# Selecting source rows with wide one-hot streams and a transpose, for fifteen groups of edges

## Time and profile before

| | |
|---|---|
| Time, median of 3 runs | 1214.72 us (1213.41 to 1215.13) |
| Span of the profiled execution, first to last instruction | 968.1 us |
| The profiled execution's own time | not given apart; the median stands for it, which leaves 246.6 us around the span |
| TensorE (PE) busy | 920.9 us, 8724 matmul passes |
| VectorE (DVE) busy | 504.3 us |
| ScalarE (ACT) busy | 247.8 us |
| GpSimd (POOL) busy | 375.2 us |
| Mean granted TensorE clock | 0.978 of 2.4 GHz |

### The profile page before, as it was taken

One profiled execution on the slowest core, in us unless ns is written; L12 is line 12 of the kernel. 1 busy time (PEld: TensorE's weight loads), 2 busy tenths in 40 slices (PEclk: granted clock), 3 DMA queues, 4 the chain that ended last, 5 costly groups with the idle time before them and its releaser, 6 DMA issues.

```text
span 968.1 us, 22399 instructions
## 1 busy us (share of the span) xinstructions
PE 920.9 (95%) x8724; PEld 699.7 (72%) x8724; DVE 504.3 (52%) x1959; ACT 247.8 (26%) x434; POOL 375.2 (39%) x398
## 2 busy tenths in 40 slices
PE   4888999999899999999889999999999999999995
PEld 2644555555454465555589999999998998999994
DVE  8699999993211111121267554554654553644541
ACT  3667677772010111001101111111111111110211
POOL 1000000000000000111277777777777777777771
PEclk9979999999999999999989999999999999999997
DMA  4300100102000000000084444444443443533430
GB/s 129 73 2 12 14 2 13 13 13 65 1 1 1 1 1 7 15 11 12 21 188 141 129 118 119 129 119 115 131 123 104 128 130 107 150 108 107 127 99 30
DMA packets 47481, 67.99 MB, mean 70 GB/s; under 512 B 15793, under 2 KB 26252, under 8 KB 47244
## 3 DMA queue, kind: packets, MB, share of 16 engines
q1 hardware_dynamic: 35852, 42.90, 16.0%
q0 software_dynamic: 11520, 23.62, 9.4%
HBM read 63.18 MB, written 3.30 MB: 69 GB/s over the span
## 4 chain that ended last, share of the span: by engine, by line
PE 84%; DVE 11%; ACT 1%; issue 1%; DMA 1%; SPq 0%; ACTq 0%; DVEq 0%
PE f_ps L1185 26%; PE f_ps L1236 25%; PE f_ps L1290 12%; PE f_ps L1221 10%; DVE f_region L611 2%; DVE f_region L609 2%; PE f_ps L1070 2%; PE f_ps L1063 2%; PE f_ps L1160 2%; DVE f_region L615 2%; DVE f_region L613 2%; PE f_ps L1122 1%; PE f_ps L1081 1%; PE f_ps L1258 1%; PE f_ps L1262 1%
## 5 line engine op out<-in xcount | busy, mean ns | idle before, releaser
L559 POOL DMA_INDIRECT f_adj<-table,f_table_idx x360 | 353.7, 982 | 110.0 <-issue 108.5
L1185 PE MATMUL f_ps<-f_adj,f_parts 125*128 125x500 fp8e4 (+1 forms) x1575 | 333.3, 353 | 0.1
L1236 PE MATMUL f_ps<-f_parts 125*128 125x128 bf16 x4200 | 250.7, 220 | 4.0 <-DVE f_parts L801 4.0
L1236 PEld LDWEIGHTS f_ps<-f_parts 125*128 125x128 bf16 x4200 | 244.0, 98 | 11.1 <-issue 8.7
L1185 PEld LDWEIGHTS f_ps<-f_adj,f_parts 125*128 125x128 bf16 x1575 | 144.0, 97 | 131.0 <-issue 13.0
L544 POOL TENSOR_TENSOR f_rest<-f_region,f_parts 125x512 f32<-125x512 f32 (+1 forms) x7 | 7.3, 1049 | 462.2 <-ACT f_parts L1028 462.2
L940 ACT CAST f_adj<-f_ps 128x500 f32 x213 | 125.9, 591 | 55.5 <-PE f_ps L1070 39.6
L1290 PE MATMUL f_ps<-f_adj 128*128 128x94 f32 (+20 forms) x984 | 128.0, 275 | 3.5 <-ACT f_adj L1050 3.5
L1290 PEld LDWEIGHTS f_ps<-f_adj 128*128 128x128 f32 x984 | 118.3, 192 | 6.0 <-issue 5.8
L781 DVE TENSOR_SCALAR f_adj<-f_iota,f_dst_abs 128x94 f32<-128x94 f16 (+4 forms) x416 | 87.7, 284 | 65.0 <-PE f_ps L1290 65.0
L1221 PE MATMUL f_ps<-f_We,f_region 128*128 128x128 f32 x832 | 114.9, 282 | 0.8 <-DVE f_region L713 0.8
(11 more groups left out here) (135 smaller groups left out, 478.4 us busy)
## 6 DMA issues: line engine op xcount, KB each, us to landing
f_region<-in_edge_attr_T SPq DMA_DIRECT2D x103, 256.0 KB
f_adj<-table,f_table_idx POOLq DMA_INDIRECT x360
f_parts<-in_src_row SPq DMA_DIRECT2D x14, 256.0 KB, 4.2
f_adj<-inv SPq DMA_DIRECT2D x1, 1562.5 KB, 8.1
table<-f_region SPq DMA_DIRECT2D x6, 250.0 KB
out<-f_xT SPq DMA_DIRECT2D x6, 250.0 KB, 2.5
f_rcntT<-inv SPq DMA_DIRECT2D x5, 250.0 KB, 3.8
f_xT<-in_xT SPq DMA_DIRECT2D x1, 812.5 KB, 6.1
```

Of the source, the lines that this page charges most:

```text
L559: pool.indirect_dma_start(out=rows[:, r % RW, j * D:(j + 1) * D], out_offset=None, in_=table, in_offset=bass.IndirectOffsetOnAxis(ap=table ...
L1185: ins = pe.matmul(ps[:, dense_ps(i):dense_ps(i) + width(c)], parts[0:NP, (l % 2) * 3 + p, b, :], adj[0:NP, b, lo:hi].bitcast(F8), start=b ...
L1236: ins = pe.matmul(z_ps(g, j), select[0:NP, u % SELECT, j * P:(j + 1) * P], parts[0:NP, 3 + p, b, :], start=b == 0 and j == 0 and p == 0, s ...
```

## The change

The selections of a picked group are turned round. In `take_sources` the table's part (125 x 128) is the weights and the 512 one-hot columns of the group are streamed, three matmuls for a unit in place of twelve. The sums then stand transposed in the bank, features on partitions and edges along the columns. So `mix` of a picked group streams `edge_attr` (512 columns) past `We1` as weights, in the same layout. ScalarE applies the Gelu into a new tile `flipping` (semaphore `smooth`), TensorE transposes its four blocks back into the same bank (`flip`, semaphore `flipped`), and ScalarE copies the result to `msg`. For group h the flip stands in iteration h - 1, so `selections` ends the units at iteration h - 2. And `SHARES` goes from 14 to 15 picked groups: 3, 9, 16, 23, 29, 36, 43, 50, 56, 63, 70, 76, 83, 90, 97, with 5 to 7 units in each iteration that has any (12 and 13 in iterations 0 and 1) and none in iterations h - 1 and h. 356 tiles are gathered in place of 360.

```diff
--- before.py
+++ after.py
@@ -56,7 +56,7 @@
         self.window = [(max(0, int(min(g * self.SLOPE, self.LAST)) - self.MARGIN - 1),
                         min(n_nodes, int((g + 1) * self.SLOPE) + self.MARGIN + 3)) for g in range(self.FG)]
         self.W = max(hi - lo for lo, hi in self.window)
-        self.SHARES = 14
+        self.SHARES = 15
         reach = self.FG - 2 * self.FTG
         self.picked = [self.FTG - 1 + i * (reach - self.FTG + 1) // (self.SHARES - 1) for i in range(self.SHARES)]
         self.node_group = [max(g for g in range(self.FG) if self.window[g][0] < e) for e in self.node_end]
@@ -90,8 +90,8 @@
         out = []
         for i, h in enumerate(self.picked):
             first = self.picked[i - 1] + 1 if i else 0
-            if first <= g < h:
-                n = h - first
+            if first <= g < h - 1:
+                n = h - 1 - first
                 out += [(i, b) for b in range((g - first) * self.NB // n, (g - first + 1) * self.NB // n)]
         return out
 
@@ -308,6 +308,7 @@
         select = spare[:, 0:SELECT * T * P].rearrange("p (a n) -> p a n", n=T * P)
         src_rows = spare[:, SELECT * T * P:(SELECT + 4) * T * P].bitcast(I32).rearrange("p (a n) -> p a n", n=T * P)
         offset = spare[:, (SELECT + 4) * T * P:(SELECT + 6) * T * P].bitcast(F16).rearrange("p (a n) -> p a n", n=T * P)
+        flipping = sb("flipping", [P, T * P])
         place_i, place = sb("place_i", [P, 1], I32), sb("place", [P, 1])
         std0, shift0 = sb("std0", [P, NB]), sb("shift0", [P, NB])
         cinv, rstd = sb("cinv", [P, NB]), sb("rstd", [P, NB])
@@ -350,6 +351,7 @@
             sem("node_added"), sem("stored"))
         tile_in, dst_tile_in, abs_ready = sem("tile_in"), sem("dst_tile_in"), sem("abs_ready")
         order_in, checked, flagged, be2_ready = sem("order_in"), sem("checked"), sem("flagged"), sem("be2_ready")
+        smooth, flipped = sem("smooth"), sem("flipped")
         cleared, repeats = sem("cleared"), sem("repeats")
 
 
@@ -408,6 +410,9 @@
         def z_group(g):
             o = (ZS if g in s.picked else s.by_rows(g) % ZS) * BANK
             return ps[:, o:o + s.tiles(g) * D]
+
+        def z_columns(g):
+            return ps[:, ZS * BANK:ZS * BANK + s.tiles(g) * P]
 
         def edge_columns(g):
             return t["edge_attr_T"][:, s.tile(g) * P:s.tile(g + 1) * P]
@@ -1036,18 +1041,21 @@
                 for c in node_due(g, ACTIVE):
                     act.wait_ge(up_mixed, c + 1)
                     act.activation(at(hT, c), node_ps(c, 1), ACT.Gelu, bias=col["bu1"][:, 0:1]).then_inc(up_active, 1)
+                if g + 1 in s.picked:
+                    act.wait_ge(z_ready, g + 2)
+                    act.wait_ge(selected, NB * (s.picked.index(g + 1) + 1))
+                    act.activation(flipping[:, :], z_columns(g + 1), ACT.Gelu).then_inc(smooth, 1)
                 if g < G:
                     w = s.tiles(g) * D
+                    if g >= MS:
+                        act.wait_ge(agg_done, g - MS + 1)
                     if g in s.picked:
-                        act.wait_ge(z_ready, g + 1)
-                        act.wait_ge(selected, NB * (s.picked.index(g) + 1))
-                        summands = z_group(g)
+                        act.wait_ge(flipped, s.picked.index(g) + 1)
+                        act.copy(msg[:, g % MS, 0:w], z_group(g)).then_inc(msg_ready, 1)
                     else:
                         act.wait_ge(pre_ready, s.by_rows(g) + 1)
-                        summands = pre[:, s.by_rows(g) % PR, 0:w]
-                    if g >= MS:
-                        act.wait_ge(agg_done, g - MS + 1)
-                    act.activation(msg[:, g % MS, 0:w], summands, ACT.Gelu).then_inc(msg_ready, 1)
+                        act.activation(msg[:, g % MS, 0:w], pre[:, s.by_rows(g) % PR, 0:w], ACT.Gelu
+                                       ).then_inc(msg_ready, 1)
 
         @block.tensor
         def _(pe):
@@ -1217,9 +1225,13 @@
                     pe.wait_ge(pre_ready, r - ZS + 1)
                 else:
                     pe.wait_ge(rows_kept, NC)
+                if held:
+                    pe.matmul(z_columns(g), weights["We1"][:, :], ea[:, g % EA, 0:T * P], start=False, stop=False,
+                              skip_group_check=True).then_inc(z_ready, 1)
+                    return
                 for j in range(s.tiles(g)):
                     ins = pe.matmul(z_ps(g, j), ea[:, g % EA, j * P:(j + 1) * P], weights["We1"][:, :],
-                                    start=not held, stop=not held, skip_group_check=held)
+                                    start=True, stop=True)
                 ins.then_inc(z_ready, 1)
 
             def take_sources(i, b):
@@ -1231,12 +1243,17 @@
                         pe.wait_ge(lowest3, NC)
                         pe.wait_ge(rows_kept, NC)
                 pe.wait_ge(select_ready, u + 1)
+                for p in range(3):
+                    ins = pe.matmul(z_columns(g), parts[0:NP, 3 + p, b, :], select[0:NP, u % SELECT, :],
+                                    start=b == 0 and p == 0, stop=b == NB - 1 and p == 2, skip_group_check=True)
+                ins.then_inc(selected, 1)
+
+            def flip(i):
+                g = s.picked[i]
+                pe.wait_ge(smooth, i + 1)
                 for j in range(T):
-                    for p in range(3):
-                        ins = pe.matmul(z_ps(g, j), select[0:NP, u % SELECT, j * P:(j + 1) * P], parts[0:NP, 3 + p, b, :],
-                                        start=b == 0 and j == 0 and p == 0, stop=b == NB - 1 and p == 2,
-                                        skip_group_check=True)
-                ins.then_inc(selected, 1)
+                    ins = pe.transpose(z_ps(g, j), flipping[:, j * P:(j + 1) * P], ident[:, :])
+                ins.then_inc(flipped, 1)
 
             def node_mix(c):
                 lo, hi = s.cols(c)
@@ -1278,6 +1295,8 @@
                     node_down(c)
                 for i, b in s.selections(g):
                     take_sources(i, b)
+                if g + 1 in s.picked:
+                    flip(s.picked.index(g + 1))
                 if g < G:
                     pe.wait_ge(oh_ready, g + 1)
                     pe.wait_ge(msg_ready, g + 1)
```

## The result

Predicted: 1229.8 us, slower by 15 us, range 1226 to 1237. Measured: **1123.62 us** (median of six runs, 1113.98 to 1128.56) against 1214.93 us before (1200.35 to 1221.08), ratio **0.927, interval 0.9235 to 0.9308**. The changed kernel is 7% faster; the prediction had the wrong sign and the wrong size.

What follows compares the result with a forecast made beforehand. TensorE (PE) was taken to bound the edge pass; -7.9 + 16.2 + 7.5 - 0.8 = +15.0 us made the span 983.1 us, and with 246.6 us around it kept, the time 1229.8 us, range 1226 to 1237.

Steps and rivals of the forecast that it cites:

- rival E: Time outside the profiled span moves as PE's program shrinks; a tenth off would give about 1205 us; chance 2%.
- Units: Selection matmuls of 14 groups, three of 512 columns replacing twelve of 128: 0.648 against 0.670 us a unit, -7.9 us.
- rival C: Successive 512-column selection matmuls overlap until weight loads set the spacing: 133 us less, 1097 us; chance 1%.
- Flip: Four fp32 transposes on TensorE for each of 15 picked groups, one pass each: 0.50 us a group, +7.5 us.
- rival D: TensorE's clock falls to 1.2 GHz after each group's transposes: about 50 us more, 1280 us; chance 1%.
- We1 for a picked group: edge_attr times We1: eight passes of 0.92 us become two of 512 columns, 0.87 us; -0.8 us over 15.
- ScalarE's two steps: Gelu into the new tile, then a copy, per picked group: both hidden behind PE's work; net 0, bound +3 us.
- rival B: PE meets ScalarE's new Gelu or copy unhidden in each of 15 groups: 15 to 30 us more; chance 5%.
- Rival A: GpSimd's gathers bound the edge pass, so four fewer give back 5.2 us: 1209.5 us, faster; chance 5%.

Runs made afterwards that it cites:

- before again: The kernel of before run once more, no edit, with a profile of its own, in a disturbed session: 1210.67 us, ratio 1.0016, span 1193.7 us.

## Why the prediction was wrong, point by point

**The step that failed: "what lies around the span is not timed by itself in what is shown, so I keep it as it is, 1214.7 - 968.1 = 246.6 us".** I treated the 246.6 us as a constant outside the span, and gave its moving 2% (rival E). All but some 2 us of it was loss inside the edge pass of the timed runs, which the profiled run did not have: 2 us lie around the span of before too (1195.84 against 1193.7). The loss is larger where the same columns take more instructions of TensorE, and this change cuts them, from 8724 to 5619 matmuls. Between the two kinds of session before differs by 1208.5 - 970.5 = 238 us, the changed kernel by 1123.6 - 980.6 = 143 us. Everything else in the prediction argued from an execution that was not like those timed. Rival E named the right place, with no mechanism and a tenth of the amount, 25 us.

**"So every microsecond of matmul added to or taken from PE's program here should appear in the time."** True in quiet sessions while the gathers keep up (15 and 20 groups), and false in disturbed ones: 14 and 15 groups take the same there, and 12 take no less.

**The terms**, as the quiet session shows them:
- Units: predicted 0.648 us, measured 0.648. Right, and with it that nothing overlaps further (rival C). The Trainium skill's 131 ns for N=512 ("TensorE: Matmul & The Clock Gate", "Back-to-back issue gap") does not hold here: 3.24 us for 15 is 216 ns.
- Flip: predicted 0.50, measured 0.44 us, -0.9 us over 15. One pass each, as taken from the earlier trace rows. The clock stayed at 1.00 from 510 to 940 us (rival D did not come). It does fall in disturbed sessions, but behind slow starts, and in before, which has no flips, too.
- We1 for a picked group: two passes, 0.89 us by their starts, near the 0.87 predicted.
- ScalarE's two steps: hidden as argued. In the quiet trace PE's idle time before the flip (L1255) was 0.7 us in all (rival B did not come).
- Missed: the aggregation's first fp32 pass. The eight passes take 0.92 us behind a unit of 128-column bf16 matmuls, and 0.86 behind a unit of 512-column ones or behind fp32 passes. Before, 84 iterations had units ahead of the aggregation and paid that; now none does: some -4.5 us.
- Together 15.0 - 0.9 - 4.5 = 9.6 us, and the measured difference is 980.6 - 970.9 = 9.7 us. That it fits to 0.1 us is luck: the medians of before alone differ by 0.4 us from one quiet session to the other. So the forecast of "slower" came true in a kind of session that its 1214.72 us did not come from.

**Rival A, the gathers**: at 15 groups they do not set the pace in a quiet session (PE busy 428.43 of 430 us). At 14 they begin to, in the tail, and at 10 they do altogether.

**What stays open.** What makes a session disturbed: nothing here could switch it.

How a gather of GpSimd delays TensorE's starts. They are not confined to moments when a gather is under way: in the trace of before again, from 530 us to the last gather, starts over 0.55 us apart fill 22% of the time with a gather running and 21% of the rest; in the changed kernel's first trace it is 14% and 22%. Slow loading of TensorE's own instructions would be a rival, but the traces do not show it. The instruction loads of 16 KB in the edge pass take 0.99 us in the median in the trace of before and 0.98 in before again, and there are 51 of them in each. No run tested it.

And why 12 to 15 groups cost the same in such a session. Fewer groups mean more gathers, but at 129 us for 332 gathers, 0.39 us each, twelve more would take back only 5 of the 51 us of TensorE's work that three groups are. What the traces show is that the slow starts grow: between 530 us and the last gather, starts over 0.55 us apart fill 99 us with 15 groups, 119 with 14 and 157 with 12 (one trace each), though TensorE has the fewest instructions with 12. So the count of instructions is not all that sets the loss.

## What to carry to other kernels

Compare the span of a profile with the time of the runs before reading anything else in it: here a difference of 246.6 us, where 2 us are usual, said that the profiled execution was another kind of run, and what its busiest engine showed was not all that the timed runs waited for. Where GpSimd issues many indirect DMAs beside a long stream of TensorE instructions, count TensorE's instructions as well as its columns, and look at the granted clock behind each gap; in this kernel the same columns in a quarter of the matmuls were worth 7% in one kind of session and nearly nothing in the other. Compare versions in both kinds before choosing.

## What the runs showed of the hardware that was not expected

- In disturbed sessions TensorE starts instructions some 0.7 us apart for stretches of a few to 20 us, only in the part of the kernel with gathers; without most of the gathers 1206 us become 995. Gathers of half the bytes (12.61 MB in place of 23.62) cost the same.
- Behind such a stretch the granted clock is 0.50, and the matmuls that follow closely take about twice as long: 105 ns each in a row of 128-column ones, 56 ns at full clock. That is some 57 us of the loss in before again.
- The price of an added matmul there was 27 to 39 ns beyond its columns. In quiet sessions 12 matmuls of 128 columns take 0.670 us and 3 of 512 take 0.648, some 2.5 ns for each added one.
- Eight fp32 passes of the aggregation behind a run of 128-column bf16 matmuls take 0.92 us, behind 512-column ones 0.86 us.
- fp32 transposes of 128 x 128 take 0.11 us each in a row (0.44 us for four) and leave the granted clock at 1.00.
